# Bilinear feature interaction on one core: output row pairs on 100 partitions against row pairs spread over all 128

## The reference, cut to what matters

```python
# feature: (2048, 200, 64)   weight: (200, 64, 64)   out: (2048, 200, 200), all fp32
bilinear = jnp.einsum('bie,ied->bid', feature, weight)
out      = jnp.einsum('bid,bjd->bij', bilinear, feature)
```

## Time and profile before

| | us |
|---|---|
| median of 3 runs | 1464.77 (1463.12 to 1466.21) |
| the profiled execution's own time | 1466.7 |
| its span, first to last instruction | 1464.8 |

### The profile page before, as it was taken

How to read it: one execution, slowest core, us unless ns; L and a number is a source line. 1 busy time by engine, 2 the same in 40 slices (tenths; PEclk the granted TensorE clock), 3 DMA queues, 4 the chain that set the end, 5 groups by cost and what they waited for, 6 DMA issues and landing times.

```text
span 1464.8 us, 40028 instructions
## 1 busy us (share of the span) xinstructions
PE 1402.8 (96%) x16192; PEld 1219.5 (83%) x16192; DVE 1167.1 (80%) x2048; ACT 831.2 (57%) x929; POOL 294.9 (20%) x518
## 2 busy tenths in 40 slices
PE   6999999999999999999999999999999999999975
PEld 5888888888888888888888888888888888888854
DVE  0578878788887888878887788877888788887897
ACT  4565565656655566555655556555565555655532
POOL 0112222122122222222221122212222122221222
PEclk9999999999999999999999999999999999999999
DMA  9899999999999999999999999999999999999898
GB/s 221 248 301 292 312 314 301 315 295 310 313 310 300 298 308 314 307 307 296 311 298 309 317 294 307 320 308 300 293 308 306 317 314 292 319 302 314 254 274 260
DMA packets 280918, 438.58 MB, mean 299 GB/s; under 512 B 53408, under 2 KB 252064, under 8 KB 280736
## 3 DMA queue, kind: packets, MB, share of 16 engines
q1 hardware_dynamic: 256160, 422.79, 89.8%
q0 software_dynamic: 24576, 13.24, 6.2%
HBM read 108.13 MB, written 327.68 MB: 298 GB/s over the span
## 4 chain that ended last, share of the span: by engine, by line
PE 77%; DVE 16%; issue 4%; DMA 2%; SPq 0%; ACT 0%; POOLq 0%
PE ps L236 41%; PE made L220 23%; PE made L204 12%; DVE staging L266 8%; DVE win L316 4%; DVE win L323 3%; DMA x<-feature_dram 2%; DVE win L324 1%; PE ps L220 0%; PE ps L204 0%; SPq L149 0%; ACT bl L290 0%; SPq L142 0%; POOLq L60 0%; POOLq L133 0%
## 5 line engine op out<-in xcount | busy, mean ns | idle before, releaser
L236 PE MATMUL ps<-win,bl 64*100 64x200 f32 x8192 | 841.4, 345 | 39.2 <-DVE staging L266 39.1
L236 PEld LDWEIGHTS ps<-win,bl 64*100 64x100 f32 x8192 | 702.3, 207 | 131.8 <-issue 60.5
L266 DVE COPY staging<-ps 100x800 f32<-100x800 f32 x512 | 503.5, 983 | 200.6 <-PE ps L236 200.2
L266 ACT COPY staging<-ps 100x800 f32<-100x800 f32 x512 | 423.6, 827 | 368.2 <-PE ps L236 368.2
L186 POOL DMA_DIRECT2D out_dram<-staging x512 | 294.2, 575 | 1161.7 <-ACT staging L266 879.8
L220 PE MATMUL made<-xt,w 64*64 64x128 f32 x6000 | 369.9, 272 | 0.0
L220 PEld LDWEIGHTS made<-xt,w 64*64 64x64 f32 x6000 | 322.7, 133 | 42.7 <-issue 42.7
L316 DVE COPY win<-xt 128x400 f32<-128x400 f32 x512 | 275.4, 538 | 65.7 <-ACT xt L280 49.9
L290 ACT COPY bl<-made 128x1024 f32<-128x1024 f32 (+1 forms) x195 | 191.2, 980 | 195.2 <-PE made L220 195.2
L204 PE MATMUL made<-ident,x 128*128 128x128 f32 x1552 | 214.6, 281 | 10.1 <-DMA x<-feature_dram 9.1
L280 ACT COPY xt<-made 128x1024 f32<-128x1024 f32 (+1 forms) x202 | 198.2, 981 | 44.3 <-PE made L204 44.3
(11 more groups left out here) (5 smaller groups left out, 0.6 us busy)
## 6 DMA issues: line engine op xcount, KB each, us to landing
out_dram<-staging SPq DMA_DIRECT2D x1024, 300.0 KB, 5.7
x<-feature_dram SPq DMA_DIRECT2D x192, 512.0 KB, 6.4
out_dram<-staging POOLq DMA_DIRECT2D x512, 25.0 KB, 5.2
x<-feature_dram SPq DMA_DIRECT2D x16, 256.0 KB, 5.2
w<-weight_dram SPq DMA_DIRECT2D x24, 128.0 KB, 6.8
w<-weight_dram SPq DMA_DIRECT2D x2, 64.0 KB, 5.1
```

Source lines behind the costliest of these rows:

```text
L236: last = nc.tensor.matmul(ps[s % TILES][0:FH, h, F * b:F * (b + 1)], rows_of_bl(n, R * k + PB * i + b)[64 * h:64 * h + 64], win[64 * h:64 ...
L266: copy(staging[:, slot, :, :, :].rearrange("p b h j -> p h b j"), ps[s % TILES][0:FH, :, 0:PB * F].rearrange("p h (b j) -> p h b j", j=F)) ...
```

## The change

A pair number m gets a place: numbers 0 to 63 the even places 0, 2, ..., 126; numbers 64 to 95 the places 1, 5, ..., 125; numbers 96 to 99 the places 3, 7, 11, 15. The other 28 places (19, 23, ..., 127) hold no number. Both axes of `bl` are laid out by places, the batches too (for which all 128 places are in use). PE reads the whole axis of 128 places as its stationary operand, so that the result has 128 partitions, of which 28 hold nothing that is stored. `staging` and its copies get 128 partitions. `store_bl` writes a group by two copies, batches 0 to 63 and 64 to 127. The 28 unused places of the first block are zeroed once by GpSimd. SP now stores numbers 0 to 63 of each set (64 partitions, 2 batches) and, after every odd set, numbers 64 to 95 of two sets (32 partitions, 4 batches); `stage` waits for both and for the rest.

```diff
-    FA = FH // 16 * 16
+    EVENS = 64
+    FA = 96
...
-        staging = sbuf("staging", [FH, OSLOTS, PB, 2, F])
+        staging = sbuf("staging", [NB, OSLOTS, PB, 2, F])
...
+        def places(number, count=1):
+            if number < EVENS:
+                return slice(2 * number, 2 * (number + count) - 1, 2)
+            if number < FA:
+                return slice(4 * (number - EVENS) + 1, 4 * (number + count - EVENS) - 2, 4)
+            return slice(4 * (number - FA) + 3, 4 * (number + count - FA), 4)
+
         def group_of_bl(n, u):
+            at = places(8 * u, GROUPS[u])
             if n % 2 == 0:
-                return bl[:, 8 * u:8 * u + GROUPS[u], :]
-            return bl[:, :, 8 * u:8 * u + GROUPS[u]]
-
-        def rows_of_bl(n, b):
-            return bl[:, 0:FH, b] if n % 2 == 0 else bl[:, b, 0:FH]
+                return bl[:, at, 0:NB:2], bl[:, at, 1:NB:2].rearrange("p c (g j) -> p c j g", j=2)
+            return bl[:, 0:NB:2, at], bl[:, 1:NB:2, at].rearrange("p (g j) c -> p j g c", j=2)
+
+        def row_of_bl(n, b):
+            at = places(b).start
+            return bl[:, :, at] if n % 2 == 0 else bl[:, at, :]
...
-                sp.dma_start(out_v[0:FA, PB * s:PB * (s + 1), :], staging[0:FA, slot]
-                             ).then_inc(out_written[slot], 16)
+                sp.dma_start(out_v[0:EVENS, PB * s:PB * (s + 1), :], staging[places(0, EVENS), slot]
+                             ).then_inc(evens_written[slot], 16)
+                if s % 2:
+                    wait_staged(sp, s - 1)
+                    sp.dma_start(out_v[EVENS:FA, PB * (s - 1):PB * (s + 1), :],
+                                 staging[places(EVENS, FA - EVENS), slot - 1:slot + 1].rearrange("p s b h j -> p (s b) (h j)")
+                                 ).then_inc(odds_written[slot // 2], 16)
...
+            nc.gpsimd.memset(bl[:, places(FH, NB - FH), :], 0.0).then_inc(bl_cleared, 1)
...
+                if n == 0 and k == 0 and i == 0:
+                    pe.wait_ge(bl_cleared, 1)
...
-                        last = nc.tensor.matmul(ps[s % TILES][0:FH, h, F * b:F * (b + 1)],
-                                                rows_of_bl(n, R * k + PB * i + b)[64 * h:64 * h + 64],
+                        last = nc.tensor.matmul(ps[s % TILES][:, h, F * b:F * (b + 1)],
+                                                row_of_bl(n, R * k + PB * i + b)[64 * h:64 * h + 64],
...
-                engine.wait_ge(out_written[slot], 16 * used)
+                engine.wait_ge(evens_written[slot], 16 * used)
+                engine.wait_ge(odds_written[slot // 2], 16 * used)
                 engine.wait_ge(rest_written[slot // 2], 16 * used)
             copy(staging[:, slot, :, :, :].rearrange("p b h j -> p h b j"),
-                 ps[s % TILES][0:FH, :, 0:PB * F].rearrange("p h (b j) -> p h b j", j=F)
+                 ps[s % TILES][:, :, 0:PB * F].rearrange("p h (b j) -> p h b j", j=F)
...
-                nc.scalar.copy(group_of_bl(n, u), rows.rearrange(cells, b=NB)).then_inc(bl_stored, 1)
+                weighed = weighed.rearrange("p (c b) -> p c b", b=NB)
+                low, high = group_of_bl(n, u)
+                order = ("p c b -> p c b", "p c (j g) -> p c j g") if n % 2 == 0 else ("p c b -> p b c", "p c (j g) -> p j g c")
+                nc.scalar.copy(low, weighed[:, :, 0:EVENS].rearrange(order[0]))
+                nc.scalar.copy(high, weighed[:, :, EVENS:NB].rearrange(order[1], j=2)).then_inc(bl_stored, 1)
```

More of the change, by code:

```diff
@@ L41, in feature_interaction @@
     WSLOTS = 4
-    FA = FH // 16 * 16
+    EVENS = 64
+    FA = 96
     assert 2 * E == 128 and B % NB == 0 and FH % 8 == C and R == 2 * PB
-    assert PB * F <= 512 and OSLOTS % 2 == 0
+    assert PB * F <= 512 and OSLOTS % 2 == 0 and FA < FH <= NB
     feature_v = feature.rearrange("b f e -> b (f e)")
@@ L87, in feature_interaction @@
         bl_stored = sem("bl_stored")
+        bl_cleared = sem("bl_cleared")
         own_filled = sem("own_filled")
@@ L92, in feature_interaction @@
         staged_dve = sem("staged_dve")
-        out_written = [sem(f"out_written{i}") for i in range(OSLOTS)]
+        evens_written = [sem(f"evens_written{i}") for i in range(OSLOTS)]
+        odds_written = [sem(f"odds_written{i}") for i in range(OSLOTS // 2)]
         rest_written = [sem(f"rest_written{i}") for i in range(OSLOTS // 2)]
@@ L169, in _ @@
                 uses = (BLOCKS * SETS_B - slot + OSLOTS - 1) // OSLOTS
-                sp.wait_ge(out_written[slot], 16 * uses)
+                sp.wait_ge(evens_written[slot], 16 * uses)
                 if slot % 2:
+                    sp.wait_ge(odds_written[slot // 2], 16 * uses)
                     sp.wait_ge(rest_written[slot // 2], 16 * uses)
@@ L186, in store_rest @@
                 nc.gpsimd.dma_start(out_v[FA:FH, PB * (s - 1):PB * (s + 1), :],
-                                    staging[FA:FH, slot - 1:slot + 1].rearrange("p s b h j -> p (s b) (h j)")
+                                    staging[places(FA, FH - FA), slot - 1:slot + 1].rearrange("p s b h j -> p (s b) (h j)")
                                     ).then_inc(rest_written[slot // 2], 16)
@@ L287, in store_bl @@
                     act.wait_ge(scores_done, (n - 1) * SETS_B + 4 * u + GROUPS[u] // 2)
-                cells = "p (c b) -> p c b" if n % 2 == 0 else "p (c b) -> p b c"
-                rows = bilinear_tile(n, u)[:].rearrange("p a c -> p (a c)")[:, 0:NB * GROUPS[u]]
-                nc.scalar.copy(group_of_bl(n, u), rows.rearrange(cells, b=NB)).then_inc(bl_stored, 1)
+                weighed = bilinear_tile(n, u)[:].rearrange("p a c -> p (a c)")[:, 0:NB * GROUPS[u]]
+                weighed = weighed.rearrange("p (c b) -> p c b", b=NB)
[3 more added lines that the diff above has]
+                nc.scalar.copy(high, weighed[:, :, EVENS:NB].rearrange(order[1], j=2)).then_inc(bl_stored, 1)
             store_xt(0)
```

## The result

The changed kernel takes 1568.7 us (median of 4 runs, 1567.8 to 1570.8) against 1464.5 us: a ratio of 1.0714, with a 95% interval of 1.0701 to 1.0727. The forecast was 1552, with a range of 1485 to 1590. Its profiled execution took 1569.1 us.

A forecast was written before the change was run, and what follows sets the result against it. PE was taken to bound 15 blocks and DVE the last, with stores hidden. Terms +83 + 4 + 0 + 0 - 1, plus 1 us for ACT's last copy, made +87 on 1466.7: 1553.7, as a median 1552; range 1485 to 1590 us.

The forecast's parts named there:

- What bounds the kernel: Whole span: PE sets the pace of 15 blocks, DVE of the last; DMA looks full but stores are hidden.
- The wide operand in even blocks: PE's strided load of 128 columns outlasts the multiply: 0.219 us a step, block 100.5 us, eight blocks +83 us.
- Odd blocks: Adjacent 128-column loads hide under multiplies except at stints' starts: 0.6 us a block, +4 us for seven; block 15 +0.
- The two copies in `store_bl`: ACT's two copies take +163 ns a group, covered by its waits for PE: 0, +5 us at the high end.
- 128 partitions in copies and PSUM, the clearing, the added wait: Wider copies and products, GpSimd's early clearing and PE's wait at L236: 0, ends -1 and +2 us for the partitions.
- Stores: SP's 512 more issues fit in its waits, 0; at the end stores land sooner, 1 us gained, ends 0 and 4.
- A: Rival, PE's loads: a full 128-column load takes a quick form, -20 us, 1445 us; chance 0.14.
- B: Rival, PE's steps in even blocks: they grow by less than the load, 1490 to 1525 us, far end 1475; chance 0.06.
- C: Rival, SP's store issues become the bound: 1478 us at 0.805 us an issue, 1777 at 1.0; chance 0.04.
- D: Rival, stores were the pace and relieved ports give time back in odd blocks: at most 4 us; no case of its own.
- The sum: Whole kernel: +87 us on the profiled 1466.7 gives 1553.7, as a median 1552; likeliest case 1525 to 1577, chance 0.76.

The follow-up runs named there:

- the last kernels above: Kernel before, last block only: L323 and L324 moved from DVE to ACT, 1465.3 us; that plus spread layout, 1456.8 us; spread layout without the move, 1464.2 us.

## Why the prediction was right, and where it was off

- **What bounds the kernel.** Right: PE in 15 blocks, DVE in the last. That the full-looking DMA share was no bound is shown by the changed kernel, which moved the same bytes with quicker stores and got nothing for it but 3 us at the end, and by the last kernels above: stores bind only once DVE doesn't.
- **The wide operand in even blocks.** The mechanism and the size held: I put 0.219 us a step, and it is 0.220; 2.07 us for 16 multiplies, 2.09; +83 us, and alone it gave +82 in even blocks (eight of them, most at 100.4 against 90.2). That the whole came out within 1 us is in part luck, as errors inside cancel. I counted the first interval of each stint twice, as a longer step and as a longer first load; it grew once, from 0.333 to 0.379 us (1.2 us a block too much). PE's drain before another tile shape, which I had put at nothing, grew from 0.263 to 0.312 us (26 x 0.05 = 1.3 us a block too little). And 1.6 us of longer steps were hidden in waits where I had put 1.2.
- **Odd blocks.** The loads were right (186 ns for 187, 1.63 us for 1.62), and each first multiply grew by the 24 ns put (410 to 434). But the wide operand alone cost an odd block 0.2 us and not 0.6: PE came later to the stint that opens block 5 and waited less there (4.26 us from first to last start for 4.65).
- **The two copies in `store_bl`.** This is the term that was mis-sized, beyond its own bounds: 0, at most +5 us, against 16 us in odd blocks (measured by reordering the copy) and some 6 in even ones. The bound on the copy itself was good, 588 to 1176 ns; it took 591 to 1171. The yardstick for its cover was wrong. I set ACT's work in four sets against their duration, a balance of throughput. What counts is one path: product done, two copies, next transposes, with two sets of PE beside it. It begins 0.1 us after the two sets do, takes 1.6 us with the slow copy, and PE starts 0.14 us behind it: 1.86 us, where the two sets and the drain are 1.56. With the one copy of 1.01 us it had been 1.3. The prediction held this path against two quick copies (1.2 us), but not against its own bound for slow ones, up to 2.4 us.
- **128 partitions in copies and PSUM, the clearing, the added wait.** 0, as forecast: L291's copies last 827 and 984 ns, and adjacent columns with 128 output partitions showed no loss.
- **Stores.** On the path, right: 0 in the blocks, 3 us at the end (ends 0 and 4). The reason given for SP, that issues last long only because the queue is full, was half right: the median fell, but the least duration rose to 0.60 us.
- **Rivals.** A (a quick load at full width) fell with the 310 ns. B (little slower) fell with the steps. C (SP the bound) didn't come, but was closer than I thought: by themselves the new stores run near SP's pace. D (the stores as the pace) fell: odd blocks grew, and no copy waited for a store.
- **The sum.** 1568.7 is 16.7 us above the 1552 forecast. The copies took 22.7 us where 1 had been put (+21.7), the width 83.7 for 87 (-3.3), the start and the end gave 3.9 for 1 (-2.9), and the medians differ by 1.5 us more than the forecast took (+1.5, of which nothing is made). That is 17.0. The total stayed within its range because the one large term was right, not because the copies were.
- **For whoever checks the rows.** Most references of the prediction from the earlier trace rows on name the group before the one meant: the two sets of blocks 4 and 5 are the earlier trace rows, the timeline 6, the other loads 7, the copies 8, SP's issues 9, the page's queues 10. The 206 ns of the memset, the first set's start at 53.5, the last multiply's at 1454.8 and the 0.83 us of ACT's copy to `staging` stand in no group, but in the trace of the kernel before.

## What to carry to other kernels

Where a weight load hides under a multiply, compare its read with the multiply's time before widening it; if the stationary columns lie apart (512 bytes here), count each twice. The lists of waits, not the share of busy time, say whether transfers bind: these ran at 0.97 of the DMA engines with no copy waiting, and making them an eighth quicker gave 2 to 3 us at the very end and nothing more until the engine ahead of them was relieved. When a copy on a side engine is split, follow the one path from its input to whoever asks for its output, and not the engine's balance; and order its elements so that the step of its writes is small.

## What the hardware showed that I had not expected

- A stationary read at a step of 512 bytes takes 1.7 ns a column, twice the 0.83 of adjacent ones, both where it is exposed (first multiplies of up to 494 and 541 ns at 100 and 128 columns) and as a step (0.173 and 0.220 us). The records of the loads in between are longer (252 and 310 ns) and overstate the difference. Its length also delays a change of tile shape behind it: 0.26 us from the last start to the next at 84 and 100 columns, 0.28 at 112, 0.31 at 128.
- ACT writes to SBUF at a step of 2 fp32 elements at full pace (583 to 630 ns for 512) and at a step of 4 at half (1082 to 1171 ns), while a step of 32 in the PSUM read costs nothing.
- SP's least issue time depends on the form of the DMA and not on the number of descriptors: 317 ns for 96 partitions by 2, 600 for 64 by 2 (595 packed). Packed, 32 partitions by 4 took 315 ns at least, and spread over every fourth partition 602. What decides this is open.
- Stores of 1600-byte rows go at 243 GB/s in DMAs of 64 and 32 partitions that lie together, at 312 in the same DMAs spread over the 128, and at 272 in DMAs of 96 together.
